# Attention with 16 heads of 8: one exponential over two score banks a step, four score banks in pairs, and the bank of the side work lent to the row-maximum units

## The reference

```
Q = (x @ Wq.T).reshape(B, xN, NUM_HEADS, HEAD_DIM)
KV = (z @ Wkv.T).reshape(B, zN, 2, NUM_HEADS, HEAD_DIM)
K = KV[:, :, 0]
V = KV[:, :, 1]
attn = jnp.einsum('bqhd,bkhd->bhqk', Q, K) * SCALE
attn = jax.nn.softmax(attn, axis=-1)
O = jnp.einsum('bhqk,bkhd->bqhd', attn, V).reshape(B, xN, DIM)
return O @ Wo.T
```

## Time and profile before

| what | us |
|---|---|
| three runs, median (lowest to highest) | 8027.38 (8024.2 to 8045.86) |
| the profiled execution's own time | 8022.59 |
| its span, from the first to the last instruction | 8020.8 |
| busy: PE, DVE, ACT | 7135.1, 5918.4, 4951.6 |
| exponentials of these stages (ACT, L687), 5,248 | 2821.7 |
| reductions of the units (DVE, L746), 4,608 | 2004.0 + 1050.2 |

### The profile page before, as it was taken

One profiled execution on the slowest core, in us unless ns is written; L12 is line 12 of the kernel. 1 busy time (PEld: TensorE's weight loads), 2 busy tenths in 40 slices (PEclk: granted clock), 3 DMA queues, 4 the chain that ended last, 5 costly groups with the idle time before them and its releaser, 6 DMA issues. The chain is left out here.

```text
span 8020.8 us, 186125 instructions
## 1 busy us (share of the span) xinstructions
PE 7135.1 (89%) x73814; PEld 3142.3 (39%) x73814; DVE 5918.4 (74%) x12885; ACT 4951.6 (62%) x9846; POOL 2313.2 (29%) x2368
## 2 busy tenths in 40 slices
PE   6999999878999997888599999999998779999979
PEld 2333333353333333444244444444444533333335
DVE  6888888657989996677466666666665469899855
ACT  4778887636888884444255555555554248888852
POOL 1222222111121110444245444544444211221200
PEclk9999999888999998788699999999999779999989
DMA  4444333114433421000100000000000144434400
GB/s 97 101 95 92 83 83 92 45 26 100 99 89 77 99 65 31 15 16 13 53 6 8 7 6 10 6 10 6 7 3 18 49 83 96 96 84 85 97 22 14
DMA packets 319828, 417.80 MB, mean 52 GB/s; under 512 B 56533, under 2 KB 238053, under 8 KB 318968
## 3 DMA queue, kind: packets, MB, share of 16 engines
q1 hardware_dynamic: 317432, 405.36, 22.4%
q10 hardware_dynamic: 1536, 0.53, 0.0%
HBM read 225.41 MB, written 174.66 MB: 50 GB/s over the span
## 5 line engine op out<-in xcount | busy, mean ns | idle before, releaser
L687 ACT ACTIVATE a_probs<-scores_ps 128x512 f32<-128x512 f32 (+2 forms) x5248 | 2821.7, 591 | 356.2 <-PE scores_ps L607 263.4
L746 DVE TENSOR_REDUCE a_unit_max<-bank 128x1 f32<-128x512 f32 x3072 | 2004.0, 684 | 182.0 <-PE bank L594 147.3
L624 PE MATMUL bank<-a_probs,a_v_sb 128*9 128x256 f32 (+1 forms) x20992 | 1614.1, 379 | 29.4 <-ACT a_out_sb L694 20.4
L1275 ACT ACTIVATE cross_probs<-scores_ps 128x512 f32<-128x512 f32 (+1 forms) x1792 | 869.4, 571 | 772.6 <-PE scores_ps L1172 772.6
L1357 DVE TENSOR_REDUCE cross_unit_max<-bank 128x1 f32<-128x512 f32 x1536 | 1006.5, 687 | 319.7 <-PE bank L1158 316.9
L607 PE MATMUL scores_ps<-a_stack 64*128 64x256 bf16 (+1 forms) x10496 | 1131.5, 275 | 61.6 <-ACT a_probs L687 55.8
L1441 POOL TENSOR_TENSOR cross_added<-cross_probs 128x1024 f32<-128x1024 f32 x384 | 902.4, 2350 | 944.6 <-PE bank L1205 868.8
L746 DVE TENSOR_REDUCE a_unit_max<-scores_ps 128x1 f32<-128x512 f32 x1536 | 1050.2, 684 | 162.1 <-PE scores_ps L594 144.6
L594 PE MATMUL bank<-a_stack 63*128 63x512 bf16 (+2 forms) x3413 | 1039.7, 372 | 8.1 <-DMA a_stack<-a_stack_dram 2.6
L607 PEld LDWEIGHTS scores_ps<-a_stack 64*128 64x128 bf16 (+1 forms) x10496 | 373.5, 96 | 991.9 <-ACT a_probs L687 832.8
L594 PE MATMUL scores_ps<-a_stack 63*128 63x512 bf16 (+2 forms) x1707 | 635.9, 373 | 50.8 <-DMA a_stack<-a_stack_dram 47.5
(11 more groups left out here) (421 smaller groups left out, 10119.5 us busy)
## 6 DMA issues: line engine op xcount, KB each, us to landing
a_stack_dram<-a_parts SPq DMA_DIRECT2D x288, 400.2 KB, 4.3
a_stack<-a_stack_dram SPq DMA_DIRECT2D x256, 348.2 KB, 8.0
a_stack<-a_stack_dram SPq DMA_DIRECT2D x128, 444.2 KB, 9.9
a_ctxT<-in_ctxT SPq DMA_DIRECT2D x48, 400.2 KB, 4.9
a_stack_dram<-a_parts SPq DMA_DIRECT2D x288, 64.0 KB, 2.7
a_stack_dram<-a_parts SPq DMA_DIRECT2D x96, 128.0 KB, 2.8
f_x<-x_after_dram SPq DMA_DIRECT2D x32, 256.0 KB, 3.6
x_after_dram<-a_res SPq DMA_DIRECT2D x48, 128.0 KB, 4.6
```

What stands on the lines that cost most here:

```text
L624: ins = pe.matmul(out_bank[32 * h:32 * h + V8, q0:TOK], v[0:n, e.t, 4 * e.g + h, :], A.probs[0:n, held, o + q0:o + TOK], start=(e.t == 0), ...
L687: act.activation(by_pair(A.probs[0:n, b, a * 512:(a + 1) * 512])[:, :, q0:TOK], by_pair(score_bank[(2 * e.i + a) % 3][0:n, :])[:, :, q0:TO ...
L746: ins = dve.tensor_reduce(unit_max[:, e.g % 2, qt, 2 * a + j, c:c + 1], bank[:, 0:e.s.chunks[c][1]], AX.X, ALU.max)
L1275: act.activation(probs[0:n, b, h, 0:m, :].rearrange("p m q -> p (m q)"), score_bank[h][0:n, 0:m * TOK], ACT.Exp, scale=scale).then_inc(S[" ...
```

## The change

- The scores have four banks, two a step, used in turn. Scores of step i wait for the exponential of step i - 2. ACT waits for both halves and takes one exponential over both banks, 1,024 columns (512 at the second tile of the own keys), and the semaphore `probs` counts one a step.
- The units keep two banks of their own (`bank2`, `bank3`). The side jobs' bank (`bank1`) is lent to the units of a step if no side job stands in the step before. Of the banks allowed, the one used longest ago is taken.
- A unit in the lent bank waits until the side jobs issued so far are done (side_done), and a side job waits until DVE has taken the last unit that was put there (max_taken).

```diff
@@ segment8
         units = units_at.get(n, [])
+        for e in units:
+            e.lent = n >= 1 and not any(job.kind in SIDE8 for job in at.get(n - 1, []))
@@ schedule8
             e.u, e.last = u, e.r == 1
+            e.bank = min(range(2 + e.lent), key=lambda bank: used[bank])
+            e.given, e.jobs = used[e.bank], n if e.bank == 2 else 0
+            used[e.bank] = u + 1
...
         if e.kind in SIDE8:
             e.n = n
+            e.back = used[2]
@@ attention8
-        score_bank = [G.S4[:, 0, 0, :], G.S4[:, 0, 1, :], G.S4[:, 1, 0, :]]
-        max_bank = [G.S4[:, 1, 1, :], G.bank[2][:, :], G.bank[3][:, :]]
+        max_bank = [G.bank[2][:, :], G.bank[3][:, :], G.bank[1][:, :]]
@@ program_pe
-                    if e.u >= 3:
-                        pe.wait_ge(S["max_taken"], e.u - 2)
+                    if e.given:
+                        pe.wait_ge(S["max_taken"], e.given)
+                    if e.jobs:
+                        pe.wait_ge(S["side_done"], e.jobs)
...
-                    if e.i >= 1:
-                        pe.wait_ge(S["probs"], 2 * e.i - 1)
+                    if e.i >= 2:
+                        pe.wait_ge(S["probs"], e.i - 1)
...
-                            ins = pe.matmul(score_bank[(2 * e.i + a) % 3][0:n, j * TOK + q0:(j + 1) * TOK],
+                            ins = pe.matmul(G.S4[0:n, e.i % 2, a, j * TOK + q0:(j + 1) * TOK],
...
                 if e.kind in SIDE8:
                     if e.n >= 1:
                         pe.wait_ge(S["side_done"], e.n)
+                    if e.back:
+                        pe.wait_ge(S["max_taken"], e.back)
@@ program_act
                     for a in range(2):
                         act.wait_ge(S[f"scores{a}"], e.i + 1)
-                        act.activation(by_pair(A.probs[0:n, b, a * 512:(a + 1) * 512])[:, :, q0:TOK],
-                                       by_pair(score_bank[(2 * e.i + a) % 3][0:n, :])[:, :, q0:TOK],
-                                       ACT.Exp, scale=A.scale).then_inc(S["probs"], 1)
+                    act.activation(by_pair(A.probs[0:n, b, :])[:, :, q0:TOK],
+                                   by_pair(G.S4[0:n, e.i % 2, :, :].rearrange("p a q -> p (a q)"))[:, :, q0:TOK],
+                                   ACT.Exp, scale=A.scale).then_inc(S["probs"], 1)
```

More of the change, by code:

```diff
@@ L210, in __init__ @@
         self.job, self.src, self.j, self.c, self.part, self.quad, self.r = job, src, j, c, part, quad, r
+        self.lent = False
 SPACE8 = 4
@@ L308, in schedule8 @@
     turns, projected, n, u, q, masked = {}, {}, 0, 0, 0, 0
-    by_row = [0, 0]
+    by_row, used = [0, 0], [0, 0, 0]
     pv_of, taken, turned_at, masked_of, emptied = {}, {}, {}, {}, {}
@@ L554, in program_sync @@
                     if e.cur >= 1:
-                        sp.wait_ge(S["probs"], 2 * steps_in * e.cur)
+                        sp.wait_ge(S["probs"], steps_in * e.cur)
                     for g in range(QUADS):
@@ L578, in program_pe @@
                         pe.wait_ge(S["stacked_rest" if e.g else "stacked_first"], (96 if e.g else 32) * (e.batch + 1))
-                    if e.u >= 3:
-                        pe.wait_ge(S["max_taken"], e.u - 2)
+                    if e.given:
+                        pe.wait_ge(S["max_taken"], e.given)
+                    if e.jobs:
+                        pe.wait_ge(S["side_done"], e.jobs)
                     qt, j, a, c = e.s.unit8(e.k)
-                    bank, c0 = max_bank[e.u % 3], q_col[idx(e)]
+                    bank, c0 = max_bank[e.bank], q_col[idx(e)]
                     if is_tail(e):
@@ L617, in program_pe @@
                     else:
-                        pe.wait_ge(S["probs"], 2 * e.i + 2)
+                        pe.wait_ge(S["probs"], e.i + 1)
                     if e.t == 0 and e.taken >= 1:
@@ L733, in program_dve @@
                     qt, j, a, c = e.s.unit8(e.k)
-                    bank = max_bank[e.u % 3]
+                    bank = max_bank[e.bank]
                     dve.wait_ge(S[f"max_scores{a}"], e.of_row + 1)
@@ L800, in program_pool @@
                     if s.mask:
-                        pool.wait_ge(S["probs"], 2 * i + 2)
+                        pool.wait_ge(S["probs"], i + 1)
                         q0 = first_query(s, e.t)
```

## The result

The changed kernel takes 8247.3 us in the median of its runs (8215.36 to 8253.57), against 8026.65 for the kernel before in the same comparison: a ratio of 1.0262, 95% interval 1.0231 to 1.0292. It is slower by 221 us; 8265 was forecast. The profiled execution, the fastest of the four, took 8215.36 us around a span of 8213.6.

A forecast was written before the change was run, and what follows sets the result against it. The prediction took DVE as the bound in a batch's later steps and PE in steps 0 to 19, ACT close behind; +131 us (a1, a3), +118 (a0) and -6 (last batches) made +243 on 8022.6, so 8265, range 8,100 to 8,390.

The forecast's parts named there:

- Four score banks: PE's waits on ACT ahead of the scores vanish: 1.2 us a batch of a1 and a3, 0.8 of a0, -51 us.
- a0's own keys: In a0, turns waiting for the last of four units and four steps between with two banks: 3.5 us a batch.
- What bounds the kernel: DVE in steps 20 to 51 of a1 (1.20 us a step), PE in steps 0 to 19, ACT close behind both.
- The exponential: One of 1,024 columns takes ACT 0.99 us against 1.16 for two: 0.17 a step, 446 us on ACT, none counted.
- The side job's wait: In a1, 0.3 us at six steps, 0.4 more at step 2, and 0.67 lost by DVE at steps 31 and 44.
- Two banks: In a1, steps 23, 36, 49 cost 0.9 us a batch, steps 6 and 10 another 0.9; a0's three tight steps 1.0.
- four steps between them with two banks: In a0, the steps between the turns of its own keys that have two banks cost 0.3 us each.
- It ends faster: Rival: side jobs' waits fall into time when PE waits anyway, leaving the gain, 7,920 to 7,972 us; chance 0.10.
- Costs and gains cancel: Rival: bank1 places cost half, tight steps nothing; +67 us, 8,090; chance 0.05 within 0.3%, 0.12 from there to 8,150.
- Two banks bind everywhere: Rival: each step not lent costs 0.3 us, 5.7 a batch of a1 and a3; near 8,500 us; chance 0.10.
- The Trainium skill's rule: Larger tiles expose less latency between instructions; with ACT as bound 446 us would come off, about 7,580; not counted.

The follow-up runs named there:

- e4: Kernel before, plus one wait: each side job waits for the unit that the changed kernel would put in the lent bank; 8229.3 us, ratio 1.0245.
- e6: Kernel before, with only the changed kernel's unit waits added (each unit waits for the one last using its bank there); 8089.0 us, ratio 1.0084.
- e7: Kernel before, with the changed kernel's waits of side jobs and of units both added, score banks and exponentials as before; 8269.6 us, ratio 1.0302.
- e5: Changed kernel, but at steps with their own side job only the step's first unit may take the lent bank; 8161.0 us, ratio 1.0176.
- e3: Changed kernel, but again two exponentials of 512 columns a step in place of one of 1,024; 8237.4 us, ratio 1.0257.
- e1: Changed kernel, but the side bank is never lent, so units always have two banks; 8469.9 us, ratio 1.0551.
- e2: Changed kernel, but the side bank is lent only where neither the step nor the one before has a side job; 8204.4 us, ratio 1.0221.

## Why the prediction was right, step by step

The waits nearly add up. In a batch of a1 the side jobs' waits cost 3.3 us (e4), the steps with two banks 1.5 (e6), together 4.6 when both are there (e7: 79.0 - 74.4), as the two overlap by 0.2 at step 6 (0.54 longer in e6, 0.31 with both). Four score banks with the long exponential give 0.8 back: 78.1. In a0: 5.6, 1.0, together 6.6, less 0.9: 97.7. The forecast's sum is nearer than its terms: costs that were too dear and a gain that was too large partly cancel, which is luck.

| term, us a batch | forecast a1 | measured a1 | forecast a0 | measured a0 |
|---|---|---|---|---|
| side jobs wait for the lent bank | 3.5 | 3.3 | 6.0 | 5.6 |
| steps with two banks | 1.8 | 1.5 | 2.2 | 1.0 |
| both together | 5.3 | 4.6 | 8.2 | 6.6 |
| four score banks in pairs | -1.2 | -0.8 | -0.8 | -0.9 |
| sum | 4.1 | 3.7 | 7.4 | 5.7 |

(The forecast for a0's own keys, 3.5, is split here into 2.3 for the turns and 1.2 for the steps between them.)

- **What bounds the kernel: right.** DVE in the later steps and PE in the first twenty. In the trace of before DVE is idle for 6.3 us a batch in steps 0 to 19 and for 0.7 in the 32 steps behind them. e5 fits this, since 0.6 us less of a wait at steps 31 and 44 comes back in full, twice a batch, but by itself it would not tell DVE from PE. ACT, said to be close behind both, was not, as the next point shows.
- **The exponential: the saving mis-sized, the conclusion right.** The prediction took 4.65 / 8 = 0.58 us for an exponential of 512 columns. But that row holds short idle times that the view merges: a pair takes less, as here in a1 of the kernel before:

```profile
2235.51 1.08 ACT L687 ACTIVATE a_probs<-scores_ps 128x512 f32<-128x512 f32 x2 [0.91 <-PE scores_ps L607]
```

Four such pairs are 4.3 us, and the rest of the 4.65 is waiting between them. Where ACT has work in hand, behind the K job, four exponentials of 512 in e3 and two of 1,024 in the changed kernel do the same work:

```profile
2259.47 2.05 ACT L697 ACTIVATE a_probs<-scores_ps 128x512 f32<-128x512 f32 x4
```

```profile
2259.23 1.93 ACT L697 ACTIVATE a_probs<-scores_ps 128x1024 f32<-128x1024 f32 x2
```

A recorded exponential lasts 0.60 and 1.02 us, so one begins (2.05 - 0.60) / 3 = 0.48 us after the other with 512 columns and 1.93 - 1.02 = 0.91 with 1,024. A step needs 0.97 us of ACT with two and 0.91 with one: it saves 0.06 us, not 0.17, and ACT stood well below the 1.20 of DVE. The busy time agrees: 2821.7 us became 2640.1, 182 less, where 446 stood. e3 shows that the saving is worth nothing here, since ACT waits for PE.
- **Four score banks: the term mis-sized.** "-32 x 1.2 - 16 x 0.8" took all of PE's waits on ACT as time of the batch. In a1 0.8 of the 1.2 came back. From e7 to the changed kernel steps 1, 3, 13, 15 and 17, each behind a side job, are 0.26 to 0.35 us shorter, 1.5 together, but the next side jobs are ready earlier and wait longer for their bank: steps 2, 4, 14, 16 and 18 are 0.8 longer.
- **The side job's wait: right in place and size, but for one.** 0.35 at three V jobs and none at the one of step 16, 0.30 at the second K job, 0.90 and not 0.87 at the output jobs. At step 2 the wait was 0.96 in the changed kernel, since the K job was itself ready earlier with the wait on ACT gone; I had 0.7, which is what e4 shows with that wait in place.
- **Two banks: right in a1, too dear in a0.** In a0 the step "four steps between them with two banks (0.3 each, as above)" failed: the waits are there, 0.23 to 0.34 each, but e6 gives 0.2 for all four where 1.2 stood, because they fall into time in which DVE still had reductions in stock. The rest of the term, 1.0 forecast, measures about 0.8.
- **The rivals.** "It ends faster" would have needed waits below 0.2 us, and "Costs and gains cancel" half the price and no tight steps; the waits were 0.30 to 0.96, and the tight steps cost 1.5. "Two banks bind everywhere" is out for the change: of its 5.7 us a batch of a1, e6 shows 1.5. It comes true once the loan goes: e1 and e2 show that the missing bank then costs as much as the side jobs' waits, or more.
- **The Trainium skill's rule** (Advanced Engine Details and Errata, The Read-Write Bubble) holds for the engine: one long exponential takes ACT 0.06 us less than two. For the kernel it gave nothing here (e3), as the engine that it spares was not the one waited for.

## What to carry to other kernels

A bank lent between two users costs the second one the time until the engine that must empty it has got through its queue up to that entry. Before lending, read off the timeline when the reader will have got to that bank, and put the loan as early in that queue as possible: two such exchanges were worth 1.2 of 78.1 us a batch of a1 here (e5). And before banks are spent on making one engine's instructions longer, ask which engine the others wait for; 0.06 us saved a step on ACT bought nothing, and giving up the units' third bank cost 1.8% in the best arrangement tried (e5) and 5.5% without a loan (e1). And before a price per instruction is read from a merged row of a timeline, see that no idle time is merged into it.

## What the runs showed of the hardware

The recorded exponentials of 512 and 1,024 columns take 597 and 1,024 ns, a slope of 0.834 ns a column, more than the 0.80 that 256 and 512 columns gave. The Trainium skill (Vector Engine (DVE) Microarchitecture Reference, Measured stream behaviour on trn2) has 0.833 ns a column for the scalar engine; the runs agree. Back to back one begins 0.48 us after the other with 512 columns (e3) and 0.91 with 1,024 (changed kernel), so the records overlap by 0.11 us at either length, and the 512 columns more cost 0.43 us, 0.84 ns each. The interval, not the recorded length, is the price.
